# A ring of four for the 0/1 adjacency, whose four operations stand in three places of a round instead of in one block

## The reference, cut to what matters

```python
def _L0_gnn_ref(x, adj, weight, bias):
    adj_norm = adj / (jnp.sum(adj, axis=-1, keepdims=True) + EPS)
    h_neigh = jnp.einsum('bnm,bmf->bnf', adj_norm, x)
    h = jnp.einsum('bnk,ko->bno', jnp.concatenate([x, h_neigh], axis=-1), weight) + bias
    return jax.nn.relu(h)

def _L1_gnn_ref(x, adj, mask, weight, w_ih, w_hh, b_ih, b_hh):
    A = (adj != 0).astype(x.dtype)
    h = x
    for l in range(weight.shape[0]):
        m = jnp.einsum('bnd,de->bne', h, weight[l])
        agg = jnp.einsum('bij,bid->bjd', A, m)
        h = _gru_cell(agg, h, w_ih, w_hh, b_ih, b_hh)
    return h * mask[..., None]

x = _layernorm(x + _L0_gnn_ref(x, adj, ...))
x = _layernorm(x + _L1_gnn_ref(x, adj, nodemask, ...))
```

## Time and profile before

| what | value |
|---|---|
| median of 3 runs | 665.11 us (664.97 to 665.69) |
| the profiled execution, its own time | 662.41 us |
| its span | 660.6 us |
| busy: TensorE products, VectorE, ScalarE, GpSimd | 617.3, 515.3, 412.0, 372.8 us |
| granted TensorE clock, mean over the span | 0.983 |
| DMA | 47.28 MB, 72 GB/s on average |

### The profile page before, as it was taken

The page is one execution under the profiler, slowest core; times in us unless marked ns, Lnnn a source line. Parts: engine busy times, 40 slices in busy tenths (PEclk is TensorE's granted clock), DMA queues, the critical chain, the costliest instruction groups (busy, mean ns, idle before and its releaser), DMA issues.

```text
span 660.6 us, 10100 instructions
## 1 busy us (share of the span) xinstructions
PE 617.3 (93%) x2922; PEld 498.4 (75%) x2922; DVE 515.3 (78%) x1153; ACT 412.0 (62%) x775; POOL 372.8 (56%) x309
## 2 busy tenths in 40 slices
PE   5689899999999999999999999999999999999973
PEld 3467678787887878787887878788787878878852
DVE  2766867879798787979878797978879797877664
ACT  4557485766757576676757666675856667555431
POOL 4425363765656576565657566565756656546252
PEclk9799999999999999999999999999999999999987
DMA  7441201222213122211312231141222211000001
GB/s 232 150 153 70 90 29 68 81 80 78 81 32 116 58 79 79 95 64 32 126 49 79 79 95 63 32 141 34 79 84 91 63 33 62 16 0 17 1 16 32
DMA packets 37423, 47.28 MB, mean 72 GB/s; under 512 B 1408, under 2 KB 18944, under 8 KB 37408
## 3 DMA queue, kind: packets, MB, share of 16 engines
q1 hardware_dynamic: 36368, 46.27, 21.3%
q10 hardware_dynamic: 944, 0.72, 0.3%
q0 software_dynamic: 96, 0.10, 0.1%
HBM read 42.90 MB, written 4.19 MB: 71 GB/s over the span
## 4 chain that ended last, share of the span: by engine, by line
PE 72%; DVE 16%; issue 4%; ACT 3%; DMA 2%; POOL 1%; DVEq 1%; POOLq 0%; SPq 0%; ACTq 0%
PE ps_tok L998 10%; PE ps_tok L1003 9%; DVE edges L730 5%; PE ps_r L890 5%; PE ps_r L892 5%; PE ps_r L891 4%; PE ps_tok L885 4%; PE ps_z L892 4%; PE ps_z L890 4%; PE ps_z L891 4%; PE ps_b L890 3%; PE ps_b L891 3%; PE ps_b L892 3%; DVE x L705 3%; PE ps_b L885 2%
## 5 line engine op out<-in xcount | busy, mean ns | idle before, releaser
L481 POOL TENSOR_TENSOR h_lo<-h,h_hi 128x512 fp32r<-128x512 f32 x64 | 83.7, 1307 | 108.6 <-ACT h_hi L518 108.6
L491 POOL TENSOR_TENSOR z_h<-z_gate,h 128x512 f32<-128x512 f32 x80 | 104.1, 1301 | 54.0 <-ACT z_gate L641 54.0
L518 ACT ACTIVATE tok_hi<-ps_tok 128x512 fp32r<-128x512 f32 x64 | 38.3, 598 | 103.6 <-PE ps_tok L885 103.5
L998 PE MATMUL ps_tok<-edges,tok_hi 128*128 (+1 forms) x320 | 91.0, 407 | 9.8 <-DVE edges L730 7.8
L434 POOL TENSOR_TENSOR adjt_lo<-adjt_in,adjt_hi 128x512 fp32r<-128x512 f32 x64 | 82.0, 1304 | 30.3 <-ACT adjt_hi L518 30.3
L871 DVE SCALAR_TENSOR_TENSOR r_hn<-ps_hn,gru_bias,r_gate 128x512 f32<-128x512 f32 x80 | 59.9, 749 | 45.0 <-ACT r_gate L631 43.7
L569 ACT ACTIVATE ps_in<-ps_in,gru_bias 128x512 f32<-128x512 f32 x80 | 52.8, 660 | 63.5 <-DVE ps_in L771 63.5
L1003 PE MATMUL ps_tok<-edges,tok_lo 128*128 (+1 forms) x320 | 88.7, 400 | 0.0
L998 PEld LDWEIGHTS ps_tok<-edges,tok_hi 128*128 128x128 f32 x320 | 59.8, 191 | 28.9 <-issue 12.6
L1003 PEld LDWEIGHTS ps_tok<-edges,tok_lo 128*128 128x128 f32 x320 | 61.1, 191 | 14.8
L804 DVE SCALAR_TENSOR_TENSOR ps_in<-z_gate,ps_in 128x512 f32<-128x512 f32 x80 | 55.1, 689 | 19.6 <-ACT ps_in L569 18.5
(11 more groups left out here) (123 smaller groups left out, 1583.3 us busy)
## 6 DMA issues: line engine op xcount, KB each, us to landing
adjt_in<-in_adj_t_dram SPq DMA_DIRECT2D x16, 1024.0 KB, 5.3
adj_in<-in_adj_dram SPq DMA_DIRECT2D x16, 1024.0 KB, 5.3
xt_in<-in_x_t_dram SPq DMA_DIRECT2D x16, 256.0 KB, 2.7
x_in<-in_x_dram SPq DMA_DIRECT2D x16, 256.0 KB, 2.8
out_dram<-y_out SPq DMA_DIRECT2D x16, 256.0 KB, 2.3
wl_t<-in_wl_t_dram ACTq DMA_DIRECT2D x1, 320.0 KB, 5.6
wih_t<-in_w_ih_t_dram ACTq DMA_DIRECT2D x1, 192.0 KB, 3.0
whh_t<-in_w_hh_t_dram ACTq DMA_DIRECT2D x1, 192.0 KB, 8.5
```

Of the source, the lines that this page charges most:

```text
L481: nc.gpsimd.tensor_tensor(h_lo[made][:], h[made][:], raw(h_hi[made][:]), ALU.subtract).then_inc(s_h_lo, 1)
L491: nc.gpsimd.tensor_tensor(z_h[:], z_gate[:], h[layer][:], ALU.mult).then_inc(s_zh, 1)
L518: return nc.scalar.activation(dst, src, ACT.Copy)
L998: nc.tensor.matmul(ps_tok[:], tok_hi[:, c * P:(c + 1) * P], edges_from(c, unit[0]), start=c == 0, stop=False)
```

## The change

`edges` gets a fourth place (8 KB more per partition), and the four operations of a round stand in three places: chunks 0 and 1 in slot 1 behind `row_inv` and ahead of `r_hn`; chunk 2 in slot 2 behind the `ps_in` add (L771) and ahead of L804; chunk 3 in slot 2 behind `mean_parts` and ahead of `tok_lo`. The wait ahead of them is now for the last layer of batch n-3, which was in slot 2 of the round before. The ramps are as they were. On TensorE only the ring's arithmetic changes (the number modulo 4 in place of 3); instructions of TensorE, ScalarE, GpSimd and the DMA queue stand in the same order as before.

```diff
-        RING, KEPT = 3, 4
+        RING, KEPT = 4, 4
...
+                        if slot == 2 and not w.ramps():
+                            edges_of((2,))
...
                         if slot == 2 and not w.leads():
                             mean_parts()
+                            if not w.ramps():
+                                edges_of((3,))
                         if slot == 3 and not w.ramps():
                             moments1()
-                        if slot == 4 and not w.ramps():
-
-                            dve.wait_ge(s_agg, w.units(LAST + 1))
-                            edges_of(range(C))
...
                             nc.vector.reciprocal(row_inv[:], row_eps[:]).then_inc(s_rinv, 1)
+                            if not w.ramps():
+                                if w.first >= 3:
+                                    dve.wait_ge(s_agg, w.last_layers())
+                                edges_of((0, 1))
...
-                ring = [pe.snap(w.batch(back) % RING) if w.first - back >= 0 else None for back in range(RING)]
+                ring = [pe.snap(w.batch(back) % RING) if w.first - back >= 0 else None for back in range(3)]
```

## The result

The change takes 653.19 us (median of 4 runs, 652.10 to 654.43); before 665.04 us (4 runs, 663.09 to 665.69). The ratio is 0.9823, with a 95% interval of 0.9800 to 0.9847: faster by 11.85 us. The prediction was 653.9 us, with 651.5 to 661.5.

A forecast was written before the change was run, and what follows sets the result against it. TensorE bounds the kernel, its products busy 617.3 of 660.6 us, so its gaps count whole. Removing its waits on `edges`, 12 x 0.88 + 0.65 = 11.2 us, gives 665.11 - 11.2 = 653.9 us, range 651.5 to 661.5.

The forecast's parts named there:

- The gap was worth 11.2 us: TensorE's 13 waits on `edges` at slot 0: 12 x 0.88 + 0.65 us saved by removing them.
- Slot 0 keeps up: In slot 0 nothing else is late: `xt_lo` goes ahead of `z_h`, `agg_lo` is in time by half a microsecond.
- Rival A: GpSimd's `z_h` goes ahead of `xt_lo` in slot 0: gain only 4.4 us, time 660.7 us; chance 0.15.
- The reading of the old block: Slot 4's four `edges` operations take 2.80 us: the third 1.52 us, the other three some 0.4 each.
- The new places cost nothing: In slots 1 and 2 the moved operations cost TensorE's path nothing; margins fall to 0.2 to 1 us.
- Rival B: TensorE's own branch and register instructions make the gap, so moving `edges` gains nothing: 665.1 us; chance 0.05.
- Rival C: GpSimd keeps the port, holding chunk 2 in slot 2 until 373.7: 4.4 us slower, 669.5 us; chance 0.06.
- the first two: The rivals said to turn on which engine goes next when both wait; in listed order, Rival A and Rival B.
- The 2.4 us for the fall of the clock near the end: The granted clock's fall near the end may move when all ends earlier: up to 2.4 us either way.
- The DMA queue: The load into `adj_in` starts more than a slot earlier, beside that of `x_in`; costed at nothing.

The follow-up runs named there:

- Experiment 1: Against the kernel before: `edges` gets a ring of four, the four operations stay as one block in slot 4; 664.28 us, ratio 0.9996.
- experiments 3 to 6: Four other placements of the four operations, one with a ring of three, against the changed kernel; 653.62, 654.75, 654.02 and 653.76 us.
- experiment 2: Against the changed kernel: only chunk 0 stands in slot 1, chunks 1 to 3 are back in slot 4; 662.20 us, ratio 0.9961.
- experiment 5: Against the changed kernel: all four operations in slot 2 behind the `ps_in` add; 654.02 us, ratio 0.9837.
- experiment 7: Against the changed kernel: all four operations in slot 1 behind `r_hn`, ahead of slot 2's `ps_in` add; 668.10 us, ratio 1.0028.
- Experiment 3: Against the changed kernel: chunks 0 and 1 stay in slot 1, chunks 2 and 3 are back in slot 4; 653.62 us, ratio 0.9839.

## Why the prediction was right, step by step

- **The gap was worth 11.2 us.** Right, 11.24 us in the steady stretch. The round went from 38.3 to 37.4 us (two rounds between 310.38 and 385.24). Experiment 1 shows that the ring has no share, and experiments 3 to 6, with the operations in four other arrangements, give the same stretch within 0.3 us, so none of it hangs on the three places as such.
- **Slot 0 keeps up.** Right. `r_hn` 347.33 for a `r_gate` done at 347.30, `h_lo` unstretched at 1.30, `xt_lo` ahead of `z_h`. Rival A did not happen here, but its mechanism is real: experiment 2 shows it where `xt_lo` asks 0.19 us too late. The margin in the changed kernel is as small as I had said, 349.16 - 348.95 = 0.21 us.
- **The reading of the old block was a little off.** I gave the three operations beside the third some 0.4 us each. The first took 0.69, held by GpSimd's `tok_lo` until 349.70. The sum does not use this, and is not changed by it:

```profile
349.31 0.69 DVE L730 TENSOR_SCALAR edges<-adj_in 128x512 f32 x1
```

```profile
348.42 1.28 POOL L472 TENSOR_TENSOR tok_lo<-x,tok_hi 128x512 fp32r<-128x512 f32 x1 [1.69 <-ACT tok_hi L518]
```

- **The new places cost nothing.** Right. Chunk 0 was held by `h_lo`, chunk 2 by `z_h`, chunks 1 and 3 ran free. `r_hn` began 0.26 us behind the end of `r_gate`, near the 0.22 forecast; L806 and `tok_lo` waited for ScalarE alone, and TensorE felt none of it.
- **Rival B** (the loop's own overhead) falls: the gap is gone in the loop, and in experiment 1 it stays with the block.
- **Rival C** failed in its working, though its chance was small. I let `rstd` hold the port for its 1.0 us; experiment 5 shows that it does not, so chunk 2 could not have been held by it from 371.62 to 372.63. The end of the path that C named, from L804 on, is the right one, and experiment 7 pays 14.1 us on it. The rivals that turn on who goes next when both engines wait are A and C; the prediction says "the first two".
- **The 2.4 us for the fall of the clock near the end** was not needed in the median. The runs of a kernel spread by about 2 to 6 us; in the two profiles above 1.5 us of it lies in the first 90 us, with a lower granted clock, which I had not named as a place of it.
- **The DMA queue.** The load into `adj_in` now starts at 337.44, right behind that of `x_in` (336.90), and no engine of the rounds waits for it. Experiment 3 leaves it waiting for slot 4's operations (it starts at 346.76, near the slot's end), and its steady stretch is the same within 0.3 us: when the load starts has no share in the gain.

**What stays open.** I did not try to take the four operations' neighbour on GpSimd away, so how much of the old gap was the meeting with GpSimd (about 1.1 of the block's 2.80 us with `h_lo`, 0.3 with `tok_lo`) and how much the mere four operations rests on the rows. The share of the held operation in the loss of experiment 7 is an estimate too. By experiment 3 two operations in that place cost nothing.

## What to carry to other kernels

Where one engine is busy nearly all the time, look for its few gaps, take each one's whole cost (here 0.88 us for 0.61 us idle: 0.77 to the next start and 0.11 in its first products), and follow the releaser back. Work moved away needs idle time on its engine at the very place where it is put, with room for an operation that the other engine holds: the same four operations cost nothing ahead of `r_hn`, where the engine was idle, and 14 us behind it, where it was not. Before paying for another buffer, see whether the old one is free soon enough: a ring of three did as well here.

## What the runs showed of the hardware

- An engine that waits for the port gets it between two instructions of the other, if it asked before the other's second: GpSimd between two VectorE operations (experiment 7), VectorE between two GpSimd instructions (the changed kernel, slot 0). In these two cases the one that went next had asked 0.26 us (335.21 - 334.95) and 0.21 us ahead of the other.
- This agrees with the Trainium skill (SBUF — State Buffer, section Who interferes with whom), by which issue order decides who blocks. Its sentence that the first has the pair "for the whole instruction" held for 128x512 instructions (a held VectorE operation ended 0.28 us, or 0.55 for `xt_lo`, behind GpSimd's), but not for the 128x4 `rstd` of experiment 5, beside whose 1.37 us three VectorE operations ran at their free pace.
- The runs of one kernel differ by up to 6 us (before, beside experiment 7: 662.53 to 668.65). The steady stretch differed by 0.12 us between two kernels that do the same there (549.24 and 549.12), so it could be read against an effect of a few us.
